# RoPE in a fused cross-attention kernel: halves moved by ScalarE, one 128-partition sine product on VectorE

## What is computed

```python
x = x + tanh(g_x) * xattn(layernorm(x), ctx, ctx)   # 8 batches x 128 tokens x 512
x = x + tanh(g_f) * ffn(layernorm(x))
# xattn: 32 query heads, 8 key/value heads, head size 128
q = q * cos + rotate_half(q) * sin                  # rotate_half: concat([-x2, x1])
k = k * cos + rotate_half(k) * sin
scores = where(mask == 0, -1e9, q @ k.T / sqrt(128)); attn = softmax(scores)
out = (attn @ v) @ Wo
```

## Time and profile before

| | |
|---|---|
| median of 3 runs | 700.46 us (698.74, 700.46, 700.66) |
| profiled execution: its time, and its span | 698.74 us, 698.7 us |
| TensorE busy | 97% of the span |
| VectorE, ScalarE, POOL busy | 76%, 47%, 51% |
| chain that ended last | TensorE 89%, VectorE 5%, nothing seen ("issue") 2% |
| mean granted clock of TensorE | 0.992 |

### The profile page before, as it was taken

How to read it: one execution, slowest core, us unless ns; L and a number is a source line. 1 busy time by engine, 2 the same in 40 slices (tenths; PEclk the granted TensorE clock), 3 DMA queues, 4 the chain that set the end, 5 groups by cost and what they waited for, 6 DMA issues and landing times.

```text
span 698.7 us, 11562 instructions
## 1 busy us (share of the span) xinstructions
PE 674.9 (97%) x3392; PEld 563.0 (81%) x3392; DVE 534.2 (76%) x878; ACT 330.9 (47%) x917; POOL 355.3 (51%) x298
## 2 busy tenths in 40 slices
PE   5878999999999999999999999999999999989998
PEld 4667888888888888888888888888888888868886
DVE  4987878787878788787878787878787878985433
ACT  3536453455345534553445445443545354875310
POOL 4534864486439544754475546653666446632000
PEclk9988999999999999999999999999999999999999
DMA  9700320031003100201021101210031005000002
GB/s 260 229 8 1 94 59 0 1 90 46 14 0 90 30 30 0 84 21 45 0 60 45 45 0 45 60 45 0 15 90 45 0 0 181 2 1 0 1 31 90
DMA packets 39090, 32.49 MB, mean 47 GB/s; under 512 B 4384, under 2 KB 29984, under 8 KB 39072
## 3 DMA queue, kind: packets, MB, share of 16 engines
q1 hardware_dynamic: 36320, 31.20, 14.9%
q0 software_dynamic: 384, 1.05, 0.5%
q10 hardware_dynamic: 2368, 0.01, 0.2%
HBM read 30.16 MB, written 2.10 MB: 46 GB/s over the span
## 4 chain that ended last, share of the span: by engine, by line
PE 89%; DVE 5%; issue 2%; ACT 1%; POOL 1%; DMA 1%; ACTq 0%; POOLq 0%; DVEq 0%
PE f_bank L323 12%; PE f_bank L325 11%; PE f_bank L324 11%; PE o_bank L323 9%; PE o_bank L325 9%; PE o_bank L324 9%; PE s_banks L433 6%; PE t_bank L329 4%; PE pv_bank L323 3%; PE pv_bank L325 3%; PE pv_bank L324 3%; PE s_banks L434 2%; PE pv_bank L329 1%; PE s_banks L325 1%; PE s_banks L323 1%
## 5 line engine op out<-in xcount | busy, mean ns | idle before, releaser
L686 ACT ACTIVATE prob<-prob,small 128x128 f32<-128x128 f32 x256 | 99.7, 391 | 132.1 <-DVE small L1148 132.1
L323 PE MATMUL o_bank<-wo_hi,o_hi 128*128 128x512 f32 x256 | 105.8, 413 | 0.0
L935 POOL TENSOR_TENSOR q<-t_cos,t_sin 128x512 f32<-128x512 f32 x64 | 82.4, 1289 | 45.8 <-DVE t_sin L1094 45.7
L323 PE MATMUL f_bank<-xT_hi,wq_hi 128*128 128x512 f32 x256 | 103.4, 404 | 0.9 <-ACT cT_hi L659 0.6
L325 PE MATMUL o_bank<-wo_hi,o_lo 128*128 128x512 f32 x256 | 100.4, 392 | 0.0
L325 PE MATMUL f_bank<-xT_hi,wq_lo 128*128 128x512 f32 x256 | 100.2, 391 | 0.0
L324 PE MATMUL f_bank<-xT_lo,wq_hi 128*128 128x512 f32 x256 | 100.0, 391 | 0.0
L324 PE MATMUL o_bank<-wo_lo,o_hi 128*128 128x512 f32 x256 | 100.0, 391 | 0.0
L950 POOL TENSOR_TENSOR prob<-prob,small 128x512 f32<-128x512 f32 x64 | 66.6, 1041 | 65.6 <-DVE small L1152 65.6
L659 ACT ACTIVATE o_hi<-pv_bank 128x512 fp32r<-128x512 f32 x64 | 38.2, 597 | 108.9 <-PE pv_bank L325 108.5
L1094 DVE TENSOR_TENSOR t_sin<-f_bank,rope 64x512 f32<-64x512 f32 x128 | 88.2, 689 | 1.8
(11 more groups left out here) (162 smaller groups left out, 1559.3 us busy)
## 6 DMA issues: line engine op xcount, KB each, us to landing
raw<-in_L_xattn_Wq_dram SPq DMA_DIRECT2D x32, 256.0 KB, 2.9
raw<-in_L_xattn_Wo_dram SPq DMA_DIRECT2D x32, 256.0 KB, 2.6
ctx_raw<-in_ctx_dram SPq DMA_DIRECT2D x8, 256.0 KB, 7.0
raw<-in_L_xattn_Wk_dram SPq DMA_DIRECT2D x8, 256.0 KB
raw<-in_L_xattn_Wv_dram SPq DMA_DIRECT2D x8, 256.0 KB
resid<-in_x_dram SPq DMA_DIRECT2D x8, 256.0 KB, 7.0
out_dram<-resid SPq DMA_DIRECT2D x8, 256.0 KB, 2.0
ffn_raw<-in_L_ffn_w_dram SPq DMA_DIRECT2D x7, 256.0 KB, 5.0
```

The lines of the kernel that those rows point to most:

```text
L323: nc.tensor.matmul(dst, st[0], mv_[0], start=start, stop=False)
L686: e = nc.scalar.activation(prob[:, k, h, :], prob[:, k, h, :], ACT.Exp, bias=nmin[k][:, h:h + 1], scale=-1.0, accum_out=psum_row[k][:, h:h ...
L935: nc.gpsimd.tensor_tensor(dst, t_cos[:, ts, :], t_sin[:, ts, :], ALU.add).then_inc(pool_rope, 1)
```

## The change

ScalarE gets a new step, `swap`, which copies the two halves of a block's bank to the other partitions of `t_sin`. VectorE multiplies `t_sin` in place by the sine rows, in one product over 128 partitions, and waits for `swap` alone, ahead of both its products; the waits for the block and for the slot have gone to ScalarE. The table's sign moves to the first half. On ScalarE `swap` stands at the places shown; on VectorE `recip(c, 1)` of even pairs moves ahead of `rotate(idx+1)`. `bank_free` still waits for `dve_rot`.

```diff
-    return np.ascontiguousarray(np.concatenate([c, c, s, -s], axis=1).astype(np.float32))
+    return np.ascontiguousarray(np.concatenate([c, c, -s, s], axis=1).astype(np.float32))
...
+            def swap(g, idx):
+
+                cnt, fixed = ropes_until(2 * g + idx // 6, idx % 6), isinstance(g, int)
+                bank, ts = f_bank[idx % 2], rope_slot(idx)
+                act.wait_ge(pe_block, 12 * g + idx + 1)
+                if not (fixed and cnt <= 2):
+                    act.wait_ge(pool_rope, cnt - 2)
+                nc.scalar.activation(t_sin[64:128, ts, :], bank[0:64, :], ACT.Copy)
+                nc.scalar.activation(t_sin[0:64, ts, :], bank[64:128, :], ACT.Copy).then_inc(act_swap, 1)
...
             tile_copy("rope", 1)
+            swap(0, 0)
             x_norms(0)
...
             first_chunk(5)
+            swap(0, 2)
             tile_copy("ctx", 6)
             tile_copy("ctx", 7)
+            swap(0, 3)
+            swap(0, 4)
+            swap(0, 5)
             tile_copy("rope", 2)
...
                 chunks = pair_chunks(g, c)
+                swap(g, idx - 1)
                 exps(g, c, 0)
...
                     for ch in chunks[1:2]:
                         split_chunk(*ch)
+                    swap(g, idx)
...
                 exps(g, c, 1)
+                if c % 2 == 0 and not first:
+                    swap(g, idx + 1)
                 pT_hi_copy(g, c, 0)
+                if c % 2:
+                    swap(g, idx + 1)
...
                 pT_hi_copy(g, c, 1)
+                if first:
+                    swap(g, idx + 1)
                 next_queries(g, c)
...
-                f_cnt = 12 * g + idx + 1
-                dve.wait_ge(pe_block, f_cnt)
-                cnt = ropes_until(u2, j)
-                if not (fixed and ropes_until(2 * g + idx // 6, j) <= 2):
-                    dve.wait_ge(pool_rope, cnt - 2)
+
+                dve.wait_ge(act_swap, ropes_until(u2, j))
...
                 times(t_cos[:, ts, :], bank[:, :], rope[:, 0, tk])
-                times(t_sin[64:128, ts, :], bank[0:64, :], rope[0:64, 1, tk])
-                times(t_sin[0:64, ts, :], bank[64:128, :], rope[64:128, 1, tk]).then_inc(dve_rot, 1)
+                times(t_sin[:, ts, :], t_sin[:, ts, :], rope[:, 1, tk]).then_inc(dve_rot, 1)
...
-                    else:
+                    recip(g, c, 1)
+                    if not first:
                         rotate(g, idx + 1)
-                    recip(g, c, 1)
                     pT_lo_split(g, c, 0)
```

More of the change, by code:

```diff
@@ L159, in build @@
         act_whi, pool_wlo = sems("act_whi", "pool_wlo")
-        pe_block, dve_rot, pool_rope = sems("pe_block", "dve_rot", "pool_rope")
+        pe_block, act_swap, dve_rot, pool_rope = sems("pe_block", "act_swap", "dve_rot", "pool_rope")
         act_khi, pool_klo = sems("act_khi", "pool_klo")
@@ L777, in pair @@
                 u2 = 2 * g + c // 2
+                idx = AHEAD + 3 * c
                 chunks = pair_chunks(g, c)
+                swap(g, idx - 1)
                 exps(g, c, 0)
```

## The result

The changed kernel takes 717.29 us (median of four runs, 715.51 to 719.17) against 700.18 us for the kernel before: a ratio of 1.0253, interval 1.0225 to 1.0281. It is slower by 17.1 us where 12.3 us were forecast; 717.29 lies in the range, and the direction was right. The profiled execution took 716.10 us with a span of 714.3, so 1.8 us lie around the span. The prediction took 698.74 us for the time of the execution profiled before, so that nothing lay around its span of 698.7. Other runs of that kernel have the same 1.8 us around the span (700.48 us with a span of 698.7), so it was more likely the run of 700.46; the sum of 12.3 us does not depend on it. (`bank_free` stands at line 371, not 405 as the description says.)

A forecast was written before the change was run, and what follows sets the result against it. TensorE was taken to bound the loop, VectorE the start. Even pairs 9.1, lock 0.7 (c = 2) and 1.2 (c = 1), start 1.3 sum to 12.3 us: 712.8, rounded to 712.5 us; range 704.5 to 718.5.

The forecast's parts named there:

- the c = 1 pairs: Sine product held up by POOL makes q_lo and the scores 0.15 us late, 8 times: 1.2 us.
- the start: Before the loop: first scores 1.0 us earlier, lost again in pair (0,0); net +1.3 us, bounds -1.0 and +4.2.
- What bounds, and where there is no slack: TensorE bounds the loop, so saved VectorE work gains nothing; even pairs' pv(c,0) already waits 0.13 us for pT_lo.
- The row in even pairs: Scores, minimum, exponentials, copies, two products, pT_lo in series: pv(c,0) starts 0.65 us later, 14 times, 9.1 us.
- V copy with c = 2: V copy 0.43 us late behind copies, exponentials, weight split; V transposes wait 0.4 us, inside the 0.65 us.
- The lock: VectorE's sine product, both inputs in SBUF, waits out POOL instructions: 0.7 us with c = 2, 1.2 with c = 1.
- The delay by block 8's copies: Pair (0,0): these copies stand ahead of the q_hi copies on ScalarE, so the next scores come at 66.6.
- The bound for the clock: At the start: a new pause might lower TensorE's clock to 1.2 GHz, costing some 3 us.
- No change: Rival: two copies hold ScalarE only 0.5 us, so pv waits as long as now; 701 us, chance 0.08.
- faster: Rival: a pair of copies below 0.38 us brings pT_lo forward, 14 waits vanish; 697.7 us, chance 0.06.
- The port rival: In c = 1 pairs t_sin misses one more 1.25 us POOL instruction, adding 10 us: 722 us, chance 0.08.
- The gap ahead of `pv(c,0)`: Sign in even pairs: a TensorE gap of 0.7 to 0.8 us there, ended by pT_lo.

The follow-up runs named there:

- the first: Changed kernel, but in even pairs block idx+1's copies stand behind pT_hi on ScalarE and its rotation behind pT_lo on VectorE; 712.86 us, ratio 1.0206.
- the eighth experiment: Kernel before the change, but in even pairs VectorE makes the reciprocal and pT_lo ahead of block idx+1's rotation; 697.25 us against 699.07, ratio 0.9968.
- third experiment: Changed kernel, but with c = 2 the weight split ahead of the V copy on ScalarE stands behind it; 718.13 us, ratio 1.0280.
- the second experiment: Changed kernel, but the sine product reads the PSUM bank, not the copied halves (result lacks the swap); 711.67 us, ratio 1.0189.
- the fifth experiment: Changed kernel with the edits of the first, second and third experiment together (result lacks the swap); 700.44 us against 699.07, ratio 1.0015.
- fourth experiment: Changed kernel, but one unshifted 128-partition ScalarE copy per block replaces two of 64 (result lacks the swap); 704.82 us, ratio 1.0083.

## Why the prediction was right, and where it was short

- **The sum.** The trace's 15.6 us against the forecast 12.3: the even pairs 10.5 (9.8 forecast, the lock's 0.7 with c = 2 included), the c = 1 pairs 4.2 (1.2), the start 0.6 (1.3), and 0.3 in small steps. The 1.5 us from there to 17.1 is the choice of the profiled executions (above).
- **What bounds, and where there is no slack**: right. The loop could only lose, and it lost first at `pv(c,0)`. Shown by the first and the eighth experiment.
- **The row in even pairs**: 0.65 us was forecast for each; 0.68 was measured with c = 4 (0.11 of it at the V transposes, where I had none) and 0.82 with c = 2 (0.75 forecast with the lock's 0.1). That 0.65 came out so well is in part luck, for two errors offset each other. The copies hold ScalarE 1.22 us, not 0.97, since the second starts 0.61 us after the first. VectorE's two products and `pT_lo` start 0.60 us apart, not 0.70: the old 64-partition ones made that 0.70.
- **V copy with c = 2**: 0.4 us forecast, 0.65 measured, for the same 1.22; that it lies inside the later wait is right but for 0.15 us (third experiment).
- **The lock**: the mechanism is shown by the second experiment. Its size is the term that failed: with c = 1, 0.15 us a pair was forecast (1.2 us in all) and 0.6 measured, about 4 us in the seven loop groups and nothing to speak of in pair (7,1). The copies were ready 0.35 us later than I reckoned; I costed the scores alone and not `pv(c,1)`, whose `pT_lo` stands behind the same stretched product (0.18); and the wait ahead of the scores cost 0.1 us more behind itself. POOL's second sum started at the forecast place within 0.2 us. One reading was wrong: the `q_lo` of 962 ns is not the only one that met a POOL instruction. 31 of the 32 overlap one; in the other 30 VectorE started first and took its usual 0.68 to 0.69 us.
- **The start**: +1.3 forecast, +0.58 in the profile, but in unequal clocks. The scores moved not 1.0 us ahead but 0.9 back (47.26, before 46.39), since each rotation takes longer through the copies; the following stretch ran at a better clock (granted clock 1.00 from 60 to 66 us, 0.76 in the kernel before) and gave it back. The delay by block 8's copies was forecast as 1.85 us (66.6 against 64.75) and is 2.06. The bound for the clock was 3 us; the four runs lie 3.7 apart.
- **Rivals.** No change and faster fall: the copies take 0.59 us, and `pv` waits. The port rival (one more missed POOL instruction in each c = 1 pair, 10 us more) did not come about, though the lock cost 3 us more than forecast.
- **Signs.** The gap ahead of `pv(c,0)` came; the copies last 0.59 us (0.58 forecast), sine products up to 1.69 (1.9), and two V copies lie 37.3 us apart on average (37.0). Two waits came where none was forecast: ahead of `pv(c,1)` with c = 1, and 0.1 us at the V transposes with c = 4. At `t_bank`, where I had feared POOL's normalisation, nothing above 0.03 us was added in the loop.

## What to carry to other kernels

Where one engine is busy throughout, find the waits that have no slack and trace the queue of instructions each hangs on. Load outside such a row was nearly free here (in the fifth experiment ScalarE took 94 us more for 0.25 us a group), and each instruction inside it cost its full time in each round. Replacing a PSUM operand by an SBUF one can cost more than the instruction it saves, if POOL reads SBUF at the same time. If the busiest engine waits a tenth of a microsecond in each round, try first the order of the queue of the engine that it waits for: that one edit gave 1.8 us, where the change lost 17.

## What was unexpected of the hardware

- Two ScalarE copies of 64 partitions out of PSUM start 0.61 us apart, shifted or not, where two of 128 start 0.48 to 0.49 apart (two in 1.07 us). So the two halves held ScalarE 1.22 us, where one whole copy holds it 0.48 (fourth experiment).
- A TensorE wait can cost more than itself: behind the waits ahead of `pv(c,0)` and of the scores (0.1 to 0.7 us) the next stage was another 0.08 to 0.10 us late, and removing a wait of 0.12 us gave back 0.21. The second matmul of such a `pv` starts 0.31 us after the first (279.15 and 279.46 in the kernel before), where 0.23 is usual. Behind the wait of 0.65 us ahead of the V transposes only 0.02 followed.
- A VectorE product with two SBUF inputs that meets a POOL instruction gets in between that one and the next, and is done 0.54 to 0.56 us after the first ends (31 times); POOL's next one then waits for it (two splits in 3.00 us, where two took 2.57).
